# Adding the high part of the residual on VectorE instead of by an identity matmul

## The chip, the cores and the metric

The kernel runs on one core of one Trainium2 chip. The metric is the device time of one execution in microseconds (us), the median of several runs. The names of the engines are those of the profile: PE is TensorE (PEld its weight loads), DVE is VectorE, ACT is ScalarE, POOL is GpSimd, SP is SyncE, which issues most of the plain transfers.

## The reference

Input x is 4 images of 512 channels, 32 x 32 pixels, fp32. Four layers follow each other:

```
layer 0  h = relu(bn(conv1x1 512->128)); offsets = conv3x3(h); h = deformable conv3x3(h, offsets)
         x = relu(bn(conv1x1 128->512 of relu(bn(h))) + x)
layer 1  25 local self-correlations of x, normalised; x = relu(conv1x1 (512+25)->512 of [x, correlations])
layer 2  h = relu(bn(conv1x1 512->128)); h = relu(bn(conv3x3 128->128)); x = relu(bn(conv1x1 128->512) + x)
layer 3  the same shape as layer 2 with other weights; its x is the output
```

What the change touches is the last line of layers 2 and 3: `relu(W3 h + b + x)`, 512 output channels in 4 blocks of 128, for each half (512 pixels) of the image. One block of one half is an "expand" step: 4 blocks x 2 halves x 2 layers = 16 a image, 64 in all.

## The kernel before

Values of layers 1 to 3 are kept as two fp32r parts, a high part and a low part (value minus high part); a product of two such values is three matmuls, high x high, low x high, high x low (`product`, L544 to L548). So each tile of 128 x 512 is left in this order: PE accumulates it in a PSUM bank; ACT applies scale, bias and relu into a slot of `ring` (4 slots, L806); ACT copies the slot to the high part (L810); DVE subtracts the high part from the slot to get the low part (L1069, items called "fine").

An expand step on PE is five matmuls of 128 x 128 by 512 columns: two by the identity `ident_r` (L665), which bring the high and the low part of the residual `xs` into the bank, and the three of the product. For layer 2 ACT and DVE then do the three operations above. For layer 3 there are no parts: the first half is drained by ACT alone (L806), the second half by DVE alone (L1076, bias and relu in one TENSOR_SCALAR), into a ring slot from which SP stores it.

The order of all work is written out by hand in `ROWS` (L80 to L95) and put together by `row_items` (L98). A row has steps of layers 1 to 3 of one image and, in the same row, a unit u of layer 0 of the image after it (18 units: two halves x nine taps) and possibly one output block of layer 0. Every engine walks the same list of items in this order and does its part of each, so an engine that waits in one item holds all that follow. The items of a row, in order: `weigh(u+1)` on ACT (4 tiles times a weight, L841) with `blend(u+1)` on DVE (12 operations, L1047); `outhigh` of an earlier block on ACT (L859, L862); the steps; `turn(u)` (PE transposes `samp`, L691; ACT copies to `sampT`, L847); the "fine" of the row's last step on DVE; `outlow` (DVE, L1063); `tap(u-1)` (PE, L701); `out0` (PE L711, DVE L1055). The "fine" of a step that isn't the last one of its row stands behind the step after it.

The expands of layer 2 stand in the rows `(2,0,0) (2,0,1)` with unit 11, `(2,0,2) (2,0,3)` with no unit, `(2,1,0) (2,1,1)` with unit 13, then `reduce(3,0)` with unit 14, then `(2,1,2) (2,1,3)` with no unit. `reduce(3,0)` waits for the "fine" of `(2,0,3)`, `reduce(3,1)` for that of `(2,1,3)`. The eight expands of layer 3 stand in pairs in the last four rows, each with an output block of layer 0.

POOL gathers the patches of layer 0 by indirect DMA, 4 to a unit, two units ahead, into 12 slots that blends free (L512 is its wait, L514 the gather). PE has four banks for the steps (`BANK`); a bank is free when `c_drained` of its step four earlier has come. The prologue (layer 0 of image 0) ends at about 176 us; three passes of the loop (layers 1 to 3 of images 0 to 2, beside layer 0 of images 1 to 3) run to 343, 519 and 690 us; the epilogue, layers 1 to 3 of image 3 alone, to the end.

Of the kernel before, what the change touches and what calls it, by code (L numbers as in the profile page):

```python
# [7 lines left out]
KC = C // P  # L8
HALF = HW // 2
# [43 lines left out]
BANK = [n % C_BANKS for n in TAKE]  # L53
# [134 lines left out]
def drains(ic, c):  # L188

    return ic * BANK_USES[BANK[c]] + TAKE[c] // C_BANKS + 1  # L190
# [18 lines left out]
def conv_seq_kernel(nc, x, w1t, offwt, offb, w2t, w3t, l1wt, l1gt, l2w1t, l2w2t, l2w3, l3w1t, l3w2t, l3w3,  # L209
# [17 lines left out]
    with ctx:  # L227
# [7 lines left out]
        def sem(name):  # L235
            return ctx.enter_context(nc.semaphore(name))
# [100 lines left out]
        out0_done, res_summed, res_relu, x1_high, x1_low = (  # L337
            sem(n) for n in ("out0_done", "res_summed", "res_relu", "x1_high", "x1_low"))
        ld_res = [sem(f"ld_res{n}") for n in range(RES)]
        c_done = sem("c_done")  # L340
        c_drained = [sem(f"c_drained{b}") for b in range(C_BANKS)]
        corr_step, norm_asked, norm_root, gs_done = (
            sem(n) for n in ("corr_step", "norm_asked", "norm_root", "gs_done"))
# [51 lines left out]
        def _(sp):  # L395
# [24 lines left out]
            def body(items, ib, ic):  # L420
# [3 lines left out]
                for it in items:  # L424
# [31 lines left out]
                    if it[0] == "step" and C_STEPS[it[1]][:2] == ("expand", 3):  # L456
                        _, _, h, m = C_STEPS[it[1]]
                        c = it[1]
                        sp.wait_ge(c_drained[BANK[c]], drains(ic, c) + 1)
                        sp.dma_start(out_v[ic, m, :, h * HALF:(h + 1) * HALF], slot(c))\  # L460
                          .then_inc(stored[RING_USE[c] % RING], 16)

# [80 lines left out]
        def _(pe):  # L543
# [79 lines left out]
            def step(c, ic):  # L623
# [15 lines left out]
                elif s[0] == "corrT":  # L639
                    h = s[1]  # L640
                    pe.wait_ge(gs_done, 6 * ic + 3 * h + 3)
                    for t in range(HT):
                        last = pe.transpose(ps[0:3 * PART, t * P:(t + 1) * P],
                                            gs[:, t].rearrange("p a b -> p (a b)"), ident)
                elif s[0] == "mix":
                    _, h, m = s
                    ct = STEP_AT[("corrT", h)]
                    pe.wait_ge(c_drained[BANK[ct]], drains(ic, ct) + 1)
                    last = pe.matmul(ps[:], l1g[:, m * P:(m + 1) * P], gsT[:], start=False, stop=True)
                elif s[0] == "reduce":  # L650
                    _, layer, h = s
                    source = [STEP_AT[("mix", h, m) if layer == 2 else ("expand", 2, h, m)] for m in range(KC)]
                    pe.wait_ge(fine_done, fined(ic, max(source, key=FINE_AT.get)))
                    for k in range(KC):
                        last = product(ps[:], [wr[layer][p][:, k, :] for p in range(2)],
                                       [xs[p][:, k, h * HALF:(h + 1) * HALF] for p in range(2)], k == 0, k == KC - 1)
                elif s[0] == "conv":
                    _, layer, h = s
                    pe.wait_ge(fine_done, fined(ic, STEP_AT[("reduce", layer, 1)]))
                    last = conv_taps(c, range(FIRST_TAPS, TAPS))  # L660
                elif s[0] == "expand":
                    _, layer, h, m = s
                    pe.wait_ge(fine_done, fined(ic, STEP_AT[("conv", layer, h)]))
                    for p in range(2):
                        pe.matmul(ps[:], ident_r[:], xs[p][:, m, h * HALF:(h + 1) * HALF], start=p == 0, stop=False)  # L665
                    last = product(ps[:], [we[layer][p][:, m * P:(m + 1) * P] for p in range(2)],
                                   [h2[p][:, h, :] for p in range(2)], False, True)
                last.then_inc(c_done, 1)
# [56 lines left out]
        def _(act):  # L725
            def col(n):
                return prm[:, n:n + 1]
# [39 lines left out]
            def step(c, ic):  # L767
                s = C_STEPS[c]
                ps = bank[BANK[c]]
                if s[0] == "gram":  # L770
# [9 lines left out]
                            ins.then_inc(aligned, 1)  # L780
                    ins.then_inc(c_drained[BANK[c]], 1)
                    return
                if s[:3] == ("expand", 3, 1):
                    return
                if s[0] == "corrT":
                    act.wait_ge(c_done, NC * ic + c + 1)
# [1 line left out]
                    return  # L788
                value, high, _ = split_parts(c)
                sc = 1.0  # L790
                if s[0] == "expand":
                    _, layer, h, m = s
                    b = col(L3_B3 + m) if layer == 3 else bn[:, 3, 2 + m:3 + m]
                elif s[0] == "mix":
                    _, h, m = s
                    b = col(L1_B + m)
                elif s[0] == "reduce":
# [6 lines left out]
                act.wait_ge(c_done, NC * ic + c + 1)  # L804
                shaped = ps[:] if len(value.shape) == 2 else ps[:].rearrange("p (a b) -> p a b", b=W)
                act.activation(value, shaped, ACT.Relu, bias=b, scale=sc).then_inc(c_drained[BANK[c]], 1)  # L806
                if s[:2] == ("expand", 3):
                    return
                act.wait_ge(c_drained[BANK[c]], drains(ic, c) + 1)
                act.activation(high, value, ACT.Copy).then_inc(step_high, 1)  # L810

# [65 lines left out]
        def _(dve):  # L877
# [123 lines left out]
            def body(items, ib, ic):  # L1001
                for it in items:
# [62 lines left out]
                    elif it[0] == "fine":  # L1065
                        c = it[1]
                        value, high, low = split_parts(c)
                        dve.wait_ge(step_high, len(SPLIT_STEPS) * ic + HIGH_AT[c] + 1)
                        dve.tensor_tensor(low, value, high.bitcast(fp32), ALU.subtract).then_inc(fine_done, 1)  # L1069
                    elif it[0] == "step":  # L1070
                        c = it[1]
                        s = C_STEPS[c]
                        if s[:3] == ("expand", 3, 1):
                            slot_free(dve, ic, c)
                            dve.wait_ge(c_done, NC * ic + c + 1)
                            dve.tensor_scalar(slot(c), bank[BANK[c]][:], prm[:, L3_B3 + s[3]:L3_B3 + s[3] + 1], 0.0,  # L1076
                                              ALU.add, ALU.max).then_inc(c_drained[BANK[c]], 1)
                        elif s[0] == "corrT":

                            dve.wait_ge(gsT_high, 2 * ic + s[1] + 1)  # L1080
# [66 lines left out]
```

## Time and profile before

| what | us |
|---|---|
| median of 3 runs | 770.78 |
| lowest, highest | 753.77, 781.69 |
| span of the profiled execution | 791.2 |
| PE, PEld busy in it | 626.6, 445.0 |
| DVE, ACT, POOL busy in it | 439.6, 366.1, 363.9 |

The three runs lie 28 us apart, and the profiled execution is another one, longer than each of them. Its trace shows what waits for what. "Idle before" of an instruction is time that its engine spent waiting, and the name behind the arrow is what ended it; "remote" or "another core or an unknown queue" is a wait whose release came without a recorded instruction beside it (here only one core runs).

### The profile page before, as it was taken

The page shows a single profiled execution, that of the slowest core. Times are in us where ns is not written, and L with a number is a line of the kernel's source. Part 1 is how long each engine was busy: PE and PEld are TensorE (multiplying, and loading weights), DVE is VectorE, ACT ScalarE, POOL GpSimd, SP SyncE. Part 2 cuts the span into 40 slices and gives each one's busy share as a digit, 9 for nine tenths or more (in the row PEclk, how much of TensorE's full clock was granted, in tenths as well). Part 3 has the DMA queues.
Part 4 walks back from the last instruction along what each step waited for, and adds up shares of the span by engine and source line. Part 5 has one row for each costly group of instructions (what it writes and reads, how often), then busy time and mean ns, then how long its engine had stood idle before and what let it go on. Part 6 is the DMA issues. An engine that isn't in the chain of part 4 may idle for free.

```text
span 791.2 us, 9836 instructions
## 1 busy us (share of the span) xinstructions
PE 626.6 (79%) x2560; PEld 445.0 (56%) x2560; DVE 439.6 (56%) x1295; ACT 366.1 (46%) x762; POOL 363.9 (46%) x453
## 2 busy tenths in 40 slices
PE   6659776467976878994966958995869488999988
PEld 3445362127743656682744636683647366787766
DVE  2437469762885567453964547464848276444222
ACT  3125235642642456552543366552626175545442
POOL 1485665816486863035585852044778750000000
PEclk9977795767997979997987969996979879999999
DMA  8695894516255643165264632164465630400002
GB/s 309 194 307 193 319 310 118 150 36 200 68 163 160 175 134 115 41 212 161 70 186 133 174 115 82 68 205 138 113 179 144 199 109 25 138 9 1 0 1 106
DMA packets 46947, 109.94 MB, mean 139 GB/s; under 512 B 6575, under 2 KB 14831, under 8 KB 46778
## 3 DMA queue, kind: packets, MB, share of 16 engines
q0 software_dynamic: 23040, 75.52, 32.3%
q1 hardware_dynamic: 23866, 34.00, 12.6%
q8 instruction: 11, 0.18, 0.1%
q14 instruction: 30, 0.25, 0.1%
HBM read 96.94 MB, written 12.55 MB: 138 GB/s over the span
## 4 chain that ended last, share of the span: by engine, by line
PE 50%; another core or an unknown queue 14%; issue 12%; POOL 11%; ACT 6%; DVE 4%; DMA 3%; ACTq 0%; SPq 0%; DVEq 0%; POOLq 0%
PE bank L546 10%; PE bank L548 10%; PE bank L547 10%; POOL patch L514 9%; PE bank L701 6%; PE bank L665 4%; PE bank L563 3%; PE bank L691 2%; PE bank L711 2%; ACT ring L806 2%; POOL tick L512 2%; ACT samp L841 1%; DVE samp L1047 1%; DMA patch<-patch_tables,idx 1%
## 5 line engine op out<-in xcount | busy, mean ns | idle before, releaser
L1047 DVE SCALAR_TENSOR_TENSOR samp<-patch,wgt,samp 128x128 f32<-128x128 f32 x864 | 237.1, 346 | 92.1 <-ACT samp L841 58.5
L514 POOL DMA_INDIRECT patch<-patch_tables,idx x216 | 220.2, 1019 | 50.1 <-issue 36.3
L512 POOL TENSOR_TENSOR tick<-tick 1x1 f32<-1x1 f32 x144 | 60.9, 423 | 211.2 <-DVE wgt L1031 120.6
L701 PE MATMUL bank<-sampT,w 128*128 128x512 f32 x144 | 91.1, 719 | 44.8 <-ACT sampT L847 34.5
L841 ACT ACTIVATE samp<-patch,wgt 128x128 f32<-128x128 f32 x288 | 93.5, 392 | 24.7 <-DMA patch<-patch_table,idx 16.2
L691 PE MATMUL bank<-ident_r,samp 128*128 128x128 f32 x288 | 50.7, 299 | 48.1 <-DVE samp L1047 42.3
L514 POOL DMA_INDIRECT patch<-patch_table,idx x72 | 77.0, 1070 | 16.8 <-issue 12.0
L847 ACT ACTIVATE sampT<-bank 128x512 f32<-128x512 f32 x72 | 42.2, 587 | 83.5 <-remote 46.4
L1069 DVE TENSOR_TENSOR xs_low<-ring,xs_high 128x512 fp32r<-128x512 f32 x64 | 43.1, 689 | 66.3 <-ACT xs_high L810 48.8
L806 ACT ACTIVATE ring<-bank,prm 128x512 f32<-128x512 f32 x64 | 44.2, 701 | 77.0 <-PE bank L548 29.8
L691 PEld LDWEIGHTS bank<-ident_r,samp 128*128 128x128 f32 x288 | 38.3, 153 | 71.3 <-DVE samp L1047 56.3
L546 PE MATMUL bank<-x_high,l1w_high 128*128 128x512 f32 x128 | 59.7, 466 | 10.3 <-issue 5.3
L806 ACT ACTIVATE ring<-bank,bn 128x512 f32<-128x512 f32 x48 | 34.0, 708 | 61.7 <-remote 36.0
L548 PE MATMUL bank<-x_high,l1w_low 128*128 128x512 f32 x128 | 54.3, 424 | 1.8 <-issue 1.8
L777 ACT ACTIVATE corr<-bank 32x320 f32<-32x320 f32 x64 | 27.4, 428 | 60.9 <-remote 38.7
L547 PE MATMUL bank<-x_low,l1w_high 128*128 128x512 f32 x128 | 54.3, 424 | 1.0 <-issue 1.0
L701 PEld LDWEIGHTS bank<-sampT,w 128*128 128x128 f32 x144 | 25.8, 221 | 51.4 <-ACT sampT L847 39.3
L563 PE MATMUL bank<-xa,w 128*128 128x512 f32 x64 | 37.7, 721 | 13.5 <-issue 7.9
L859 ACT ACTIVATE res<-res,prm 128x512 f32<-128x512 f32 x32 | 23.1, 721 | 48.5 <-DVE res L1055 48.4
L546 PE MATMUL bank<-x_high 128*128 128x256 f32 x128 | 37.6, 294 | 6.0 <-ACTq L869 4.1
L810 ACT ACTIVATE xs_high<-ring 128x512 fp32r<-128x512 f32 x64 | 40.4, 631 | 2.0
L548 PE MATMUL bank<-x_high,x_low 128*128 128x256 f32 x128 | 37.8, 296 | 1.4 <-issue 1.4
(168 smaller groups left out, 1214.9 us busy)
## 6 DMA issues: line engine op xcount, KB each, us to landing
res<-in_x SPq DMA_DIRECT2D x32, 256.0 KB
out_y<-ring SPq DMA_DIRECT2D x32, 256.0 KB, 2.1
xa<-in_x SPq DMA_DIRECT2D x7, 1024.0 KB, 7.3
patch<-patch_tables,idx POOLq DMA_INDIRECT x216
patch_tables<-midT SPq DMA_DIRECT2D x11, 256.0 KB
patch<-patch_table,idx POOLq DMA_INDIRECT x72
xa<-in_x SPq DMA_DIRECT2D x4, 256.0 KB, 4.9
xa<-in_l1wt SPq DMA_DIRECT2D x1, 1024.0 KB
```

Source lines behind the costliest of these rows:

```text
L512: pool.tensor_tensor(tick[:, p:p + 1], tick[:, 0:1], tick[:, 0:1], ALU.add).then_inc(ticked, 1)
L514: pool.indirect_dma_start(patch[:, n % SLOTS].rearrange("p a c -> p (a c)"), None, table, bass.IndirectOffsetOnAxis(ap=idx[:, e:e + 1], ax ...
L546: pe.matmul(ps, w[0], a[0], start=start, stop=False)
L547: pe.matmul(ps, w[0], a[1], start=False, stop=False)
L548: return pe.matmul(ps, w[1], a[0], start=False, stop=stop)
L563: last = pe.matmul(bank[h][:], w1[:, c, :], xa[i % 2][:, c, h * HALF:(h + 1) * HALF], start=c == 0, stop=c == KC - 1)
L691: last = pe.transpose(bank[4 + u % 2][:, t * P:(t + 1) * P], samp[:, u % 2, t, :], ident)
L701: pe.matmul(bank[6 + h][:], w2[:, k, :], sampT[:, u % 2, :], start=k == 0, stop=k == TAPS - 1).then_inc(tap_done, 1)
L806: act.activation(value, shaped, ACT.Relu, bias=b, scale=sc).then_inc(c_drained[BANK[c]], 1)
L841: act.activation(samp[:, u % 2, t, :], patch[:, n % SLOTS, 0, :], ACT.Copy, scale=wgt[:, (HT * h + t) * TAPS + k, 0:1]).then_inc(weighed, 1)
L1047: dve.scalar_tensor_tensor(o_, g_, w_, o_, ALU.mult, ALU.add).then_inc(blended, 1)
L1069: dve.tensor_tensor(low, value, high.bitcast(fp32), ALU.subtract).then_inc(fine_done, 1)
```

## The change

PE's expand step has four matmuls: the identity matmul for the low part alone, and the product. DVE drains the bank for all 16 expands of an image: one SCALAR_TENSOR_TENSOR adds bank, bias and the high part of the residual into the ring slot, without relu. ACT then reads the slot: for layer 2 it writes relu of it straight into the high part of `xs`; for layer 3 it applies relu in place and signals a new semaphore `final`, on which SP's store waits. The "fine" of a layer 2 expand on DVE becomes a SCALAR_TENSOR_TENSOR: max of the slot with 0, minus the high part.

```
 PE    pe.wait_ge(fine_done, fined(ic, STEP_AT[("conv", layer, h)]))
-      for p in range(2):
-          pe.matmul(ps[:], ident_r[:], xs[p][:, m, h * HALF:(h + 1) * HALF], start=p == 0, stop=False)
+      pe.matmul(ps[:], ident_r[:], xs[1][:, m, h * HALF:(h + 1) * HALF], start=True, stop=False)
 ACT
-      if s[:3] == ("expand", 3, 1):
+      if s[0] == "expand":
+          act.wait_ge(c_drained[BANK[c]], drains(ic, c) + 1)
+          if s[1] == 3:
+              act.activation(slot(c), slot(c), ACT.Relu).then_inc(final, 1)
+          else:
+              act.activation(split_parts(c)[1], slot(c), ACT.Relu).then_inc(step_high, 1)
           return
 DVE, fine
+      if C_STEPS[c][0] == "expand":
+          dve.scalar_tensor_tensor(low, value, 0.0, high.bitcast(fp32), ALU.max, ALU.subtract)\
+             .then_inc(fine_done, 1)
+      else:
           dve.tensor_tensor(low, value, high.bitcast(fp32), ALU.subtract).then_inc(fine_done, 1)
 DVE, step
-      if s[:3] == ("expand", 3, 1):
+      if s[0] == "expand":
+          _, layer, h, m = s
+          b = prm[:, L3_B3 + m:L3_B3 + m + 1] if layer == 3 else bn[:, 3, 2 + m:3 + m]
           slot_free(dve, ic, c)
           dve.wait_ge(c_done, NC * ic + c + 1)
-          dve.tensor_scalar(slot(c), bank[BANK[c]][:], prm[:, L3_B3 + s[3]:L3_B3 + s[3] + 1], 0.0,
-                            ALU.add, ALU.max).then_inc(c_drained[BANK[c]], 1)
+          dve.scalar_tensor_tensor(slot(c), bank[BANK[c]][:], b,
+                                   xs[0][:, m, h * HALF:(h + 1) * HALF].bitcast(fp32),
+                                   ALU.add, ALU.add).then_inc(c_drained[BANK[c]], 1)
 SP
-      sp.wait_ge(c_drained[BANK[c]], drains(ic, c) + 1)
+      sp.wait_ge(final, 2 * KC * ic + KC * h + m + 1)
       sp.dma_start(out_v[ic, m, :, h * HALF:(h + 1) * HALF], slot(c))
```

## Rows read from the trace of the kernel before

**Rows 1.** Page, busy us, share of the span and instructions of each engine.

```profile
PE 626.6 (79%) x2560; PEld 445.0 (56%) x2560; DVE 439.6 (56%) x1295; ACT 366.1 (46%) x762; POOL 363.9 (46%) x453
```

**Rows 2.** Chain of waits that ended last, its start and two stretches: start, us, what.

```profile
466.73 0.85 PE bank L665 x2
...
478.66 0.46 PE bank L665 x2
...
578.90 12.81 another core or an unknown queue
```

**Rows 3.** Stretches: window, us, busy of PE, PEld, DVE, ACT, POOL; clock, DMA.

```profile
612.00:636.00 24.00, 11.26 (x47) 7.81 (x46) 7.52 (x25) 5.83 (x14) 15.56 (x22) 0.83 0.61 175
636.00:652.00 16.00, 16.00 (x60) 11.54 (x59) 14.35 (x44) 13.29 (x28) 11.73 (x12) 0.83 0.43 122
744.00:792.00 48.00, 41.07 (x171) 31.53 (x169) 12.01 (x17) 19.46 (x30) 0.00 (x0) 1.00 0.12 44
```

**Rows 4.** Timeline of PE, third pass: start, us, engine, line, form, idle before.

```profile
622.57 0.60 PE L691 MATMUL bank<-ident_r,samp 128*128 128x128 f32 x4
635.50 2.08 PE L701 MATMUL bank<-sampT,w 128*128 128x512 f32 x2 [12.33 <-ACT sampT L847]
```

**Rows 5.** Groups of instructions: form, count, busy us, mean ns, idle before.

```profile
L665 PE MATMUL bank<-xs_high,ident_r 128*128 128x512 f32 x64 | 35.7, 558 | 0.1
L806 ACT ACTIVATE ring<-bank,bn 128x512 f32<-128x512 f32 x48 | 34.0, 708 | 61.7 <-remote 36.0 <-PE bank L548 23.3 <-issue 1.5
L810 ACT ACTIVATE xs_high<-ring 128x512 fp32r<-128x512 f32 x64 | 40.4, 631 | 2.0
L859 ACT ACTIVATE res<-res,prm 128x512 f32<-128x512 f32 x32 | 23.1, 721 | 48.5 <-DVE res L1055 48.4
L1055 DVE SCALAR_TENSOR_TENSOR res<-bank,prm,res 128x512 f32<-128x512 f32 x32 | 23.9, 746 | 4.8 <-PE bank L711 3.1 <-DMA res<-in_x 1.5
L1069 DVE TENSOR_TENSOR xs_low<-ring,xs_high 128x512 fp32r<-128x512 f32 x64 | 43.1, 689 | 66.3 <-ACT xs_high L810 48.8 <-issue 17.5
L1076 DVE TENSOR_SCALAR ring<-bank,prm 128x512 f32<-128x512 f32 x16 | 12.0, 751 | 7.4 <-PE bank L548 7.4
```

**Rows 6.** Timeline of DVE, second pass, blends and "fines" around the layer 2 expands.

```profile
469.29 0.69 DVE L1063 TENSOR_TENSOR x_low<-res,x_high 128x512 fp32r<-128x512 f32 x1
...
472.40 0.69 DVE L1069 TENSOR_TENSOR xs_low<-ring,xs_high 128x512 fp32r<-128x512 f32 x1 [1.43 <-issue]
473.01 3.29 DVE L1047 SCALAR_TENSOR_TENSOR samp<-patch,wgt,samp 128x128 f32<-128x128 f32 x12
476.21 1.29 DVE L1069 TENSOR_TENSOR xs_low<-ring,xs_high 128x512 fp32r<-128x512 f32 x2
477.42 3.24 DVE L1047 SCALAR_TENSOR_TENSOR samp<-patch,wgt,samp 128x128 f32<-128x128 f32 x12
480.57 0.69 DVE L1069 TENSOR_TENSOR hp_low<-ring,hp_high 128x512 fp32r<-128x512 f32 x1
```

**Rows 7.** Timeline of ACT and PE in the same stretch of the second pass.

```profile
475.92 0.58 ACT L847 ACTIVATE sampT<-bank 128x512 f32<-128x512 f32 x1
...
477.64 1.02 PE L701 MATMUL bank<-sampT,w 128*128 128x512 f32 x2
...
485.22 0.50 PE L546 MATMUL bank<-xs_high,l3w_high 128*128 128x512 f32 x1 [2.08 <-DVE xs_low L1069]
```

**Rows 8.** Timeline of PE, third pass, the last two of four output blocks of layer 0.

```profile
683.65 1.02 PE L711 MATMUL bank<-hid,w 128*128 128x512 f32 x2
686.84 1.02 PE L711 MATMUL bank<-hid,w 128*128 128x512 f32 x2
```

**Rows 9.** Timeline of the epilogue: the last layer 2 expands and the end.

```profile
761.28 0.69 DVE L1069 TENSOR_TENSOR xs_low<-ring,xs_high 128x512 fp32r<-128x512 f32 x1 [0.54 <-ACT xs_high L810]
762.12 0.47 PE L546 MATMUL bank<-xs_high,l3w_high 128*128 128x512 f32 x1 [2.57 <-DVE xs_low L1069]
...
787.83 0.75 DVE L1076 TENSOR_SCALAR ring<-bank,prm 128x512 f32<-128x512 f32 x1 [0.41 <-PE bank L548]
```

More of the change, by code:

```diff
@@ L339, in conv_seq_kernel @@
         ld_res = [sem(f"ld_res{n}") for n in range(RES)]
-        c_done = sem("c_done")
+        c_done, final = sem("c_done"), sem("final")
         c_drained = [sem(f"c_drained{b}") for b in range(C_BANKS)]
@@ L790, in step @@
                 sc = 1.0
[L791 to L794, printed above, removed]
+                if s[0] == "mix":
                     _, h, m = s
@@ L806, in step @@
                 act.activation(value, shaped, ACT.Relu, bias=b, scale=sc).then_inc(c_drained[BANK[c]], 1)
-                if s[:2] == ("expand", 3):
-                    return
                 act.wait_ge(c_drained[BANK[c]], drains(ic, c) + 1)
@@ L1068, in body @@
                         dve.wait_ge(step_high, len(SPLIT_STEPS) * ic + HIGH_AT[c] + 1)
-                        dve.tensor_tensor(low, value, high.bitcast(fp32), ALU.subtract).then_inc(fine_done, 1)
+                        if C_STEPS[c][0] == "expand":
+                            dve.scalar_tensor_tensor(low, value, 0.0, high.bitcast(fp32), ALU.max,
+                                                     ALU.subtract).then_inc(fine_done, 1)
+                        else:
+                            dve.tensor_tensor(low, value, high.bitcast(fp32), ALU.subtract).then_inc(fine_done, 1)
                     elif it[0] == "step":
```

## The prediction

> **What bounds the kernel now.** I read busy shares first: PE 79%, DVE 56%, ACT and POOL 46% [rows 1]. That says which engine to look at, not what its work is worth. The chain of waits comes next. In it the expands of layer 2 in a pass of the loop are a run of PE pieces: the two identity matmuls of one expand take 0.85 us at the half clock and 0.46 us at full clock [rows 2], so a removed one is worth 0.43 or 0.23 us where PE is the chain. But the chain also has pieces as in 578.90, 12.81 us that no recorded instruction ended [rows 2]. The stretches show where these lie: from 612 to 636 us PE is busy for 11.26 of 24 us, DVE for 7.52, ACT for 5.83, and POOL, which only issues gathers, for 15.56 [rows 3]. PE had issued the transposes of unit 12 at 622.57 and then stood for 12.33 us until ACT had copied them [rows 4]. Here PE's work costs nothing. Then 636 to 652 us: PE 16.00 of 16 us, DVE 14.35, ACT 13.29 [rows 3]. Here PE is the chain, but with DVE and ACT right behind it, and this is where six of the eight layer 2 expands lie. From 652 on, and through the epilogue, PE is mostly the chain at full clock.
>
> So the change takes work from PE and gives it to DVE at a place where DVE has 1.65 us to spare.
>
> **Part 1, PE.** 64 identity matmuls go. Their mean of 558 ns [rows 5] holds pipelining; the step between matmuls is 0.23 us, and 0.43 at half clock [rows 2]. All of them: 64 x 0.23 = 14.7 us, and 0.2 us more for each at half clock, perhaps 8 of them, 1.6 us: 16.3 us, if nothing else were late.
>
> **Part 2, the price of the new operations.** The drain on DVE is a SCALAR_TENSOR_TENSOR of 128x512 from PSUM with a second tensor from SBUF. L1055 is this very form: 746 ns [rows 5]. ACT's relu from the slot is not shown for this pair of types; the Copy L810 has 631 ns and the relu with bias L859 721 ns [rows 5]; I take 0.67. The new "fine" with max is not shown either: between the TENSOR_TENSOR, 689 ns, and L1055, 746 ns; I take 0.69, as both its inputs are in SBUF as there [rows 5]. For the three such operations that lie on the chain of one image the two ends are less than 0.2 us apart.
>
> A layer 2 expand costs before: ACT 0.71 + 0.63 and DVE 0.69; after: DVE 0.75 + 0.69 and ACT 0.67 [rows 5]. A layer 3 expand before: one drain of 0.7 (ACT in the first half, L806; DVE in the second, L1076); after: DVE 0.75 and ACT 0.67. DVE gains 12 operations an image, 12 x 0.75 x 4 = 36 us in all. The chain from c_done to the low part of a single expand stays as long as it was (0.71 + 0.63 + 0.69 against 0.75 + 0.67 + 0.69). For a pair it gets shorter: ACT was the slower one at 1.34 a tile; now DVE does drain, drain, fine, fine, 4 x 0.69 to 0.75 = 2.9 us, with ACT beside it, against 3.4. SP's wait moves from the drain to the relu; nothing but stores stands behind it.
>
> **Part 3, layer 2 in a pass.** The pair with unit 11 comes out of the stall of the gathers, and both chains have one length: nothing gained or lost. For the other three pairs I walk through DVE's list in the second pass.
> - (2,0,2), (2,0,3): before, the last fine ran from 472.40 to 473.09, and blend(14) began at 473.01 [rows 6]. DVE is free from 469.98, where its outlow ends [rows 6]. Drain, drain, fine, fine takes it to 472.8 to 473.0. Blend(14) starts where it did.
> - (2,1,0), (2,1,1): blend(14) ends at 476.3. ACT could drain these tiles during the blend; DVE can't. Two drains now stand behind it, 476.3 to 477.8, then ACT's relu to 478.4. Only behind that relu comes ACT's copy of sampT for unit 13: 478.4 to 479.0, where it ran from 475.92 to 476.50 [rows 7]. That is 2.5 us late. PE's tap 13, which began at 477.64 [rows 7], begins at 479.0, 1.4 us late, although PE saved 2 x 0.43 + 2 x 0.23 = 1.3 us before it: PE stands for 2.5 us.
> - ACT's weigh(15) follows sampT, so blend(15), which ran from 477.42 [rows 6], begins at 479.4 and ends at 482.6, and the fine of reduce(3,0) (at 480.57 before [rows 6]) ends at 483.3.
> - (2,1,2), (2,1,3): drain, drain, fine, fine, 483.3 to 486.2. reduce(3,1) begins at 486.2, where it began at 485.22 [rows 7]. **Loss 1.0 us a pass**, with every saving of PE in these rows gone into waits.
>
> In the third pass the same steps give a loss of 0.9 to 1.1.
>
> **Part 4, layer 3 in a pass.** The last four rows come 3.19 us apart [rows 8], all PE: two expands of 1.16 and an output block of 0.86. After: 2.72. DVE does two drains, an outlow and an out0 in each, 0.75 + 0.67 + 0.60 + 0.75 = 2.77, as they follow one another without a gap; ACT 2 x 0.67 + 0.72 + 0.63 = 2.7. All three level, so I take 2.8: 4 x 0.4 = **1.6 us gained a pass**. Three passes: 3 x (1.0 - 1.6) = -1.8 us.
>
> **Part 5, epilogue.** No layer 0 work covers anything here: DVE is busy for 12.01 of the last 48 us, PE for 41.07 [rows 3]. Before, reduce(3,1) started at 762.12 behind a fine that began at 761.28 [rows 9]. The same walk (PE 0.93 an expand, DVE 2.9 a pair, conv(2,1) moved up by 0.5) gives 762.4: +0.3. The conv steps don't change. The eight expands of layer 3 give 8 x 0.23 = 1.84 us back on PE. At the end a tile was out 0.75 us after its drain began (787.83 [rows 9]) and stored 2.6 us later (791.2 less 788.6); now 0.7 of relu comes between. A ring slot is then held for 0.75 + 0.7 + 2.6 = 4.0 us while PE makes four tiles in 3.7: +0.4. Sum: 0.3 - 1.84 + 0.7 + 0.4 = **-0.4 us**.
>
> **Sum.** -1.8 - 0.4 = -2.2 us of 791.2, so 789. The profiled execution is 2.6% longer than the median of 770.78, and the runs spread from 753.77 to 781.69. Scaled by 0.974: **768.6 us**, no change that could be told (I count 2%, 15.4 us, as what can be told). Bounds of this case by itself: PE's 0.23 saved on all of the passes' last rows and part of the layer 2 ones, 6 us less; the losses of part 3 without the gains of part 4, 5 us more; 763 to 776.
>
> **A rule against a row.** The share of the span is the measure by which PE at 79% comes out as the engine to relieve, and yet 636 to 652 us shows DVE at 14.35 of 16 us [rows 1, 3]. The Trainium skill, page "Perfetto Trace Analysis", section "Identifying the Most-Contended Engine", says that for TensorE the matmul busy share is no good measure and the share of weight loads is to be taken. By it PE (56%) and DVE (56%) would be level before, and after the change DVE, at about 60%, would lead: nothing gained, or something lost. The trace agrees with this where the layer 2 expands lie, and not in the last rows of a pass, where PE without a gap sets the pace.
>
> **Rivals.**
> *PE's saving gets through.* If PE is the chain nearly everywhere (its busy time is 626.6 [rows 1], and the chain has PE in every expand) and DVE's drains fit between blends, all of part 1 counts: -16.3 + 0.7 at the end = -15.6, that is 775.6, scaled 755. For it: PE without a gap from 636 to 652 [rows 3]. Against it: DVE's 14.35 there has no room for four drains, and the pair in the shadow of unit 11 is worth nothing. Chance 0.14.
>
> *Slower: PE's pauses pull its clock down.* Place: tap 13 and reduce(3,1). PE's pause before reduce(3,1) was 2.08 us, in the epilogue 2.57 [rows 7, 9], and the clock stayed at 2.4 GHz. After 12.33 us of standing it was at 1.2 GHz: identity matmuls of 0.43 us [rows 2, 4]. After the change PE stands for 2.5 us at tap 13 and for 3 to 4 us at reduce(3,1), close to each other. If this is enough, the reduce and conv steps behind it run at half speed for some time; the mean of 0.83 over 636 to 652 us [rows 3] is 1/3 of the time at half level, 5.3 us, in which 2.7 us of work are lost. Two such stretches an image, one behind each pause, with the loss of part 3 and the gain of part 4: 4 x (2 x 2.7 + 1.0 - 1.6) = 19, so 810, scaled 789; with one stretch an image 779. It decides from the point at which pauses of 3 to 4 us, not 2.6, bring the clock down. Chance 0.12.
>
> *The gaps of the gathers move.* Waits like the 12.81 us that nothing recorded ended [rows 2] come where POOL issues gathers back to back [rows 3], some two or three a pass. The change shifts blends by 2 us, and blends free the gathers' slots. One such gap more or less in one pass is 13 us; in every pass 38 us. The runs before lie 28 us apart, most likely for this reason. Nothing in the trace says to which side: 0.06 for more than 13 us faster, 0.06 for slower.
>
> *The relief of ACT counts.* ACT loses 8 operations of layer 2 and gains 4 in layer 3 an image. It leads only if ACT was the bound; its share of 46% and part 3, where it waits for DVE, speak against it. Inside the forecast's own range.
>
> **How the numbers follow.** Forecast 0.62, saving gets through 0.14, clock 0.12, gaps 0.12. Faster by over 2%: half of the case at 755, which lies on the border (0.07), the gaps to that side (0.06), and 0.03 for the spread of the runs: 0.16. Slower by over 2%: the clock case with both stretches (0.06), the gaps (0.06), 0.02 for the spread: 0.14. Within: 0.70. Range: 752 to 786, which takes in the 755 of the one rival and all but the far end of the other, and the spread of a median of such runs.
>
> **What would show it.** In the profile after: L665 with 64 instead of 128 matmuls; DVE about 473 us busy, PE about 36 less than 626.6 by the records. Step 3 is right if PE stands for 2 to 3 us before tap 13 (L701) with ACT's sampT as releaser, and reduce(3,1) waits longer than 2.08 for DVE; wrong if tap 13 comes directly behind the transposes. Step 4 is right if L711 comes 2.8 us apart in the last rows. Step 5 is right if the last store ends less than 1 us earlier, counted from reduce(2,0) of the epilogue. The clock rival shows as a granted clock under 1.00 in the 30 us behind reduce(3,1). The forecast is wrong as a whole if the last 55 us of a pass change by over 3 us.

## The result and the profile after

| set of runs | kernel before, median us | changed kernel, median us | ratio, 95% interval |
|---|---|---|---|
| first | 769.96 (753.77 to 784.88) | 769.25 (760.69 to 782.97) | 1.0124 (1.0069 to 1.0180) |
| second | 783.05 (776.13 to 794.70) | 785.79 (777.64 to 793.12) | 1.0021 (0.9976 to 1.0066) |
| third | 785.25 (775.51 to 798.33) | 784.36 (776.12 to 1412.3) | 0.9994 (0.9945 to 1.0043) |

The forecast of 768.6 us and "no change" came out in the median, and its sign did not: I had 2 us to the good; the first interval says 0.7 to 1.8% slower, the other two hold no change. The ratio of the first set compares the runs within 1.5% of the fastest of each kernel, which are 4 of 20 before and 13 of 20 after, since the kernel before spread more. The medians of all runs in it are 0.7 us apart, with the changed kernel the lower one. So no change of 2% was there, a loss of up to 1.8% may have been, and taking 64 matmuls from PE bought nothing. The page after, with its chain by engine:

```profile
PE 611.5 (80%) x2496; PEld 432.6 (56%) x2496; DVE 469.2 (61%) x1343; ACT 356.4 (46%) x746; POOL 365.9 (48%) x453
...
PE 33%; DVE 17%; issue 17%; another core or an unknown queue 10%; POOL 10%; ACT 8%; DMA 4%; DVEq 1%; SPq 0%; ACTq 0%; POOLq 0%
```

Against [rows 1], PE has 64 matmuls and 15.1 us less and DVE 29.6 us more. That is near 64 steps of 0.23 us (14.7), and not the 36 us that the prediction read off the records: PE's records overlap, and the identity matmul that is left, now the first of its group, has 554 ns where it had 411. The groups that answer to [rows 5] (form, count, busy us, mean ns, idle before):

```profile
L664 PE MATMUL bank<-xs_low,ident_r 128*128 128x512 f32 x64 | 35.5, 554 | 3.2 <-DVE h_low L1072 1.8 <-issue 1.3
L1081 DVE SCALAR_TENSOR_TENSOR ring<-bank,bn,xs_high 128x512 f32<-128x512 f32 x32 | 22.6, 742 | 8.5 <-remote 5.0 <-PE bank L548 3.4
L1069 DVE SCALAR_TENSOR_TENSOR xs_low<-ring,xs_high 128x512 fp32r<-128x512 f32 x32 | 21.7, 692 | 0.7
L787 ACT ACTIVATE xs_high<-ring 128x512 fp32r<-128x512 f32 x32 | 20.2, 631 | 45.7 <-DVE ring L1081 29.8 <-issue 15.5
L785 ACT ACTIVATE ring<-ring 128x512 f32<-128x512 f32 x32 | 18.7, 619 | 3.0 <-DVE ring L1081 2.8
```

The prices were right: drain 742 ns for 0.75, fine 692 for 0.69, relu 619 to 631 for 0.67. DVE in the second pass, where [rows 6] stood (start, us, engine, line, form):

```profile
456.77 3.23 DVE L1046 SCALAR_TENSOR_TENSOR samp<-patch,wgt,samp 128x128 f32<-128x128 f32 x12
459.92 1.40 DVE L1081 SCALAR_TENSOR_TENSOR ring<-bank,bn,xs_high 128x512 f32<-128x512 f32 x2
461.36 1.35 DVE L1069 SCALAR_TENSOR_TENSOR xs_low<-ring,xs_high 128x512 fp32r<-128x512 f32 x2
462.79 3.27 DVE L1046 SCALAR_TENSOR_TENSOR samp<-patch,wgt,samp 128x128 f32<-128x128 f32 x12
465.98 0.68 DVE L1072 TENSOR_TENSOR hp_low<-ring,hp_high 128x512 fp32r<-128x512 f32 x1
466.59 1.40 DVE L1081 SCALAR_TENSOR_TENSOR ring<-bank,bn,xs_high 128x512 f32<-128x512 f32 x2
468.02 1.35 DVE L1069 SCALAR_TENSOR_TENSOR xs_low<-ring,xs_high 128x512 fp32r<-128x512 f32 x2
```

No idle time stands in any of these rows: from 456.8 to 469.4 DVE's list is the clock of the kernel. The timelines of ACT and PE there, beside [rows 7]:

```profile
460.70 1.29 ACT L787 ACTIVATE xs_high<-ring 128x512 fp32r<-128x512 f32 x2 [3.40 <-issue]
461.89 0.58 ACT L846 ACTIVATE sampT<-bank 128x512 f32<-128x512 f32 x1
...
462.52 1.13 PE L700 MATMUL bank<-sampT,w 128*128 128x512 f32 x2 [1.81 <-DVE xs_low L1069]
...
469.43 0.50 PE L546 MATMUL bank<-xs_high,l3w_high 128*128 128x512 f32 x1 [0.93 <-DVE xs_low L1069]
```

The sampT copy stands right behind the two relus and ends at 462.47, and tap 13 starts at 462.52, with PE idle for 1.81 us, where it had come without a wait. (The row names a "fine" of DVE as the releaser; what tap 13 waits for in the program is sampT.)

A pass can be cut by rows of PE: the first matmul of the correlations (gram), of reduce(2,0), of reduce(3,0), of reduce(3,1), and gram again. Lengths of these stretches in us, three passes each, from the traces of this case:

| kernel | gram to reduce(2,0) | to reduce(3,0) | to reduce(3,1) | to gram |
|---|---|---|---|---|
| before | 62.1, 64.3, 62.9 | 59.5, 65.6, 62.6 | 11.91, 11.20, 11.21 | 34.1, 34.1, 34.0 |
| before, profile of the third set | 61.9, 63.5, 63.8 | 59.5, 59.9, 59.8 | 11.43, 11.27, 9.60 | 35.6, 35.6, 34.1 |
| changed | 60.7, 62.5, 61.3 | 59.0, 54.0, 55.0 | 12.56, 12.53, 12.58 | 33.5, 33.5, 33.4 |
| changed, second set | 61.9, 62.5, 61.8 | 60.7, 60.0, 60.5 | 12.57, 12.58, 12.58 | 33.5, 33.6, 33.5 |

Stretches one and two vary by several us from profile to profile of either kernel; that is where the 23.7 us between the two first profiles lie, and nothing is read from it. Stretch three is longer in the changed kernel every time, and always the same. Stretch four is shorter. The two values of 35.6 in the third set's profile hold a stretch of low clock right behind reduce(3,1) (granted clock 0.68 from 306.7 to 312.0 us in the first pass), to which PE came after 2.29 and 2.14 us of idle time; the changed kernel stands there for 0.93 us (second pass) and shows no low clock behind it in the nine passes of its three full profiles.

### The profile page after: what moved, and what is told of

It reads as the page before. It is cut to its first block, busy times and chain, and to the rows that moved or that the text cites. A ratio compares the mean times of both kernels' runs of the same rounds, so it can differ in the third digit from the quotient of the medians.

```text
span 767.5 us, 9731 instructions
## 1 busy us (share of the span) xinstructions
PE 611.5 (80%) x2496; PEld 432.6 (56%) x2496; DVE 469.2 (61%) x1343; ACT 356.4 (46%) x746; POOL 365.9 (48%) x453
## 3 DMA queue, kind: packets, MB, share of 16 engines
q0 software_dynamic: 23040, 75.52, 33.4%
## 4 chain that ended last, share of the span: by engine, by line
PE 33%; DVE 17%; issue 17%; another core or an unknown queue 10%; POOL 10%; ACT 8%; DMA 4%; DVEq 1%; SPq 0%; ACTq 0%; POOLq 0%
DVE samp L1046 8%; POOL patch L514 8%; PE bank L546 8%; PE bank L548 7%; PE bank L547 7%; PE bank L700 3%; PE bank L563 3%; DVE ring L1081 2%; POOL tick L512 1%; PE bank L690 1%; ACT samp L840 1%; DMA out_y<-ring 1%; PE bank L710 1%; ACT ring L807 1%
## 5 line engine op out<-in xcount | busy, mean ns | idle before, releaser
L700 PE MATMUL bank<-sampT,w 128*128 128x512 f32 x144 | 88.5, 702 | 37.2 <-ACT sampT L846 20.1
L840 ACT ACTIVATE samp<-patch,wgt 128x128 f32<-128x128 f32 x288 | 95.2, 392 | 40.4 <-DMA patch<-patch_tables,idx 19.3
L807 ACT ACTIVATE ring<-bank,prm 128x512 f32<-128x512 f32 x48 | 34.0, 709 | 42.0 <-PE bank L548 21.5
L563 PE MATMUL bank<-xa,w 128*128 128x512 f32 x64 | 34.9, 683 | 10.1 <-DMA xa<-in_x 5.9
L787 ACT ACTIVATE xs_high<-ring 128x512 fp32r<-128x512 f32 x32 | 20.2, 631 | 45.7 <-DVE ring L1081 29.8
L710 PE MATMUL bank<-hid,w 128*128 128x512 f32 x64 | 36.7, 665 | 2.6 <-DVE res L1054 1.6
L547 PE MATMUL bank<-x_low,x_high 128*128 128x256 f32 x128 | 37.6, 294 | 0.8 <-issue 0.7
```

Source lines behind the costliest of these rows:

```text
L547: pe.matmul(ps, w[0], a[1], start=False, stop=False)
L563: last = pe.matmul(bank[h][:], w1[:, c, :], xa[i % 2][:, c, h * HALF:(h + 1) * HALF], start=c == 0, stop=c == KC - 1)
L700: pe.matmul(bank[6 + h][:], w2[:, k, :], sampT[:, u % 2, :], start=k == 0, stop=k == TAPS - 1).then_inc(tap_done, 1)
L710: pe.matmul(bank[b][:], w3[:, m * P:(m + 1) * P], hid[:], start=True, stop=True)\
L840: act.activation(samp[:, u % 2, t, :], patch[:, n % SLOTS, 0, :], ACT.Copy, scale=wgt[:, (HT * h + t) * TAPS + k, 0:1]).then_inc(weighed, 1)
```

## The experiments

**1 to 4. Without the gathers.** The gathers' waits cover everything of a few us, so POOL writes ones into each slot instead of gathering; then the change, and each half of it, are timed.

```
-  pool.indirect_dma_start(patch[:, n % SLOTS]..., None, table, ...).then_inc(gathered[n % SLOTS], 16)
+  pool.memset(patch[:, n % SLOTS], 1.0).then_inc(gathered[n % SLOTS], 1)
```

The kernel before without gathers was expected so:

> The kernel before, with each gather of layer 0's patches replaced by a fill of the same slot with ones on GpSimd (this part of the result is left out; every other instruction is kept). If the waits that nothing recorded ended (13.8% of the chain, some two or three a pass) belong to the gathers, they are gone from the trace, the time falls by about 100 us from 770 to 650 to 690, and the runs lie within 3 us of each other instead of 28. If they belong to something else (code loading, ScalarE, semaphores), they stay.

The changed kernel without gathers:

> The changed kernel with the same replacement. Theory (VectorE's in-order list sets the pace of the layer 2 expands, and its lag eats most of the layer 3 gain): 2 to 5 us slower than the kernel before with the same replacement, from +1.0 to +1.7 a pass in layer 2, -0.65 a pass in layer 3 and +1.0 in the epilogue. Rival A (TensorE's saving gets through): 8 to 16 us faster. Rival B (only the gaps of the gathers moved): within 1 us.

Only the eight expands of layer 2 an image changed (each part of the diff under `if s[:2] == ("expand", 2)`):

> No gathers, and only the expands of layer 2 changed. Theory: 3 to 7 us slower than the kernel before without gathers (three passes at +1.0 to +1.7, the epilogue at 0 to +1.7 by the clock). Rival A: 6 to 8 us faster (32 matmuls at 0.23).

Only those of layer 3 changed:

> No gathers, and only the expands of layer 3 changed. Theory: 2 to 4 us faster than the kernel before without gathers (three passes at -0.7 to -1.1 since VectorE starts its drains behind a fine and an output block, the epilogue at -0.7). Rival A: 7 us faster (32 matmuls at 0.23).

Measured (stretches from the profiles), with the kernel before at 782.28 us beside them:

| without gathers | median us (lowest, highest) | reduce(2,0) to reduce(3,0) | to reduce(3,1) | to gram | epilogue |
|---|---|---|---|---|---|
| before | 637.27 (636.02, 638.34) | 36.9 | 9.23 | 34.0 | 101.1 |
| changed | 648.83 (646.96, 649.27) | 37.6 | 12.52 | 33.5 | 103.4 |
| layer 2 alone | 651.58 (650.21, 652.00) | 37.6 | 12.52 | 34.0 | 103.6 |
| layer 3 alone | 637.86 (637.62, 638.27) | 36.9 | 9.23 | 33.5 | 101.7 |

With the gathers gone the kernel before takes 637 us, below the 650 to 690 that I had expected, and its runs lie 2.3 us apart. The change costs 11.6 us (1.8%) here, all of it layer 2's. Both sizes that I gave for it, 2 to 5 and 3 to 7, were too small; layer 3 alone, from which I expected 2 to 4 us, gave nothing (0.6 us slower). The rival by which PE's saving arrives is dead: with PE at 91% of the span, it would have shown here if anywhere.

In the two profiles, which lie 13.4 us apart, the difference is 3 x 3.3 us in stretch three, 3 x 0.7 in the stretch before it, 3 x 0.5 back in the one behind it, and 2.3 in the epilogue; the rest is in the prologue and in stretch one, whose length changes with the low clock that falls into it (49.4 to 53.7 us over all profiles without gathers). Stretch three, reduce(3,0) to reduce(3,1) in the second pass, as windows (us, busy of PE, PEld, DVE, ACT, POOL; clock, DMA), first before, then changed:

```profile
357.64:366.86 9.22, 9.17 (x38) 5.95 (x37) 8.69 (x27) 8.78 (x19) 3.24 (x6) 1.00 0.00 1
```

```profile
363.42:375.95 12.53, 10.45 (x36) 6.58 (x35) 12.37 (x34) 7.13 (x17) 2.25 (x6) 0.86 0.00 0
```

Before, PE has 9.17 of 9.22 us, ACT 8.78 and DVE 8.69: three engines level. The change puts 3.7 us more on DVE there: four drains of 0.70, and 0.8 us of blend(14), which begins 0.1 us ahead of reduce(3,0) and no longer 0.9. So DVE has 12.37 of 12.53 us. (The clock of 0.86 costs nothing: the passes at full clock have 12.53 and 12.52 us too.)

**5 to 7. DVE's order, or DVE's load?** One kernel lets DVE do the drains of expand(2,1,0) and (2,1,1) ahead of blend(14):

```
+  pair = [("step", STEP_AT[("expand", 2, 1, m)]) for m in range(2)]
+  at = items.index(("blend", 14, 0));  items = items[:at] + pair + items[at:]     # DVE's list only
```

> The changed kernel, gathers replaced by a write of ones into the slot (that part of the result is left out). Only VectorE's order is changed: its two drains of the tiles of expand(2, 1, m) stand ahead of blend(14) and not behind it. Reference 648.8 us for the changed kernel and 637.3 us for the kernel before, both without gathers. Theory 'order' (TensorE waits because a drain stands behind 3.3 us of blends, then sampT(13) behind the relu): most of the +3.3 us a pass from reduce(2, 1)'s tiles to reduce(3, 1) comes back, 1.5 us a pass or more, time 644 us or less. Theory 'load' (VectorE has no idle time from the first drain of layer 2 to reduce(3, 1), so that each operation moved forward moves another back): under 0.5 us a pass, time 647 to 650 us.

Measured: 648.07 us (647.96 to 650.44), stretch three 12.14 us for 12.52. Only 0.4 us a pass came back. The other two take load away:

```
-  g_ = patch[:, (HT * u + t) % SLOTS, corner, :];    o_ = samp[:, u % 2, t, :]
+  wide_ = 8 if u in (14, 15) and corner > 1 else P
+  g_ = patch[:, (HT * u + t) % SLOTS, corner, 0:wide_];    o_ = samp[:, u % 2, t, 0:wide_]
```

> The changed kernel without gathers, 16 of its blend operations a pass narrowed from 128 to 8 columns (those of units 14 and 15, corners 2 and 3; their sum is left out of the result). Everything keeps its place and its waits; VectorE has some 2 us a pass less to do between the drains of layer 2 and reduce(3, 1). Theory 'load': time falls from 648.8 by 1.5 to 2 us a pass, to 643 or less (-5 to -7 with the prologue's and epilogue's rows). Theory 'order' with TensorE as the bound behind it: about half of that, 646 or more.

> Control for the last: the kernel before without gathers, the same 16 blend operations a pass narrowed to 8 columns. Theory 'load': in the kernel before VectorE does not set the pace between the drains of layer 2 and reduce(3, 1), so the time stays within 2 us of 637.3. If it falls by as much as the changed kernel's (5 us or more), VectorE set the pace in both and the change only lengthened its list by its own work.

Measured: changed 639.99 us (639.34 to 641.45), stretch three 10.55; before 634.71 us (633.63 to 636.68), stretch three 9.23 in all three passes, as it was. The 2.6 us that it lost on the median, 0.6 more than the 2 that I had allowed, show in its trace as the third pass, 129.7 us for 132.1, and not in the stretch of the blends: the profile of the kernel before has 6.8 us at the lower clock in stretch one of that pass, and this one has none. In the changed kernel DVE's busy time in stretch three fell by 1.97 us (12.37 to 10.40) and the stretch by 1.97; in the kernel before it is worth nothing there. (Runs 5 to 8 were taken on another chip than 1 to 4; stretch two of the changed kernel has 37.6 us on both.) The loss in stretch three is DVE's load, by experiment.

**8, 9. The clock in the epilogue.** Windows of the changed kernel without gathers, around reduce(3,1), which came behind 3.26 us of idle PE:

```profile
608.00:615.00 7.00, 4.90 (x20) 3.67 (x20) 4.87 (x9) 3.49 (x6) 0.00 (x0) 1.00 0.00 0
615.00:622.00 7.00, 5.68 (x13) 4.46 (x14) 1.18 (x2) 0.57 (x2) 0.00 (x0) 0.54 0.01 2
```

The granted clock of 0.54 is the lower level, 1.2 GHz, for nearly the whole window. The experiment gives PE something to do before that wait:

```
+  if isinstance(ic, int) and ic == N - 1 and s == ("reduce", 3, 1):
+      pe.wait_ge(sampT_done, UNITS * N)
+      for _ in range(8): pe.matmul(bank[5][:], ident_r[:], h2[0][:, 1, :], start=True, stop=True)
```

> The changed kernel without gathers, with 8 matmuls of 128x512 added in the epilogue ahead of reduce(3, 1)'s wait, in a free PSUM bank that nobody reads, so that TensorE does not stand for 3.3 us there. Theory 'clock': the stretch of 6.8 us at the lower clock behind that pause goes away, and time falls from 648.8 by 2 to 3.4 us. Rival (the stretch costs nothing, since VectorE and ScalarE end the epilogue): within 1 us of 648.8.

> The changed kernel with 8 matmuls of 128x512 added in the epilogue ahead of reduce(3, 1)'s wait, in a free PSUM bank that nobody reads. Without gathers this took away a stretch of 6.8 us at the lower clock and 2.8 us. In the first profile of the changed kernel that stretch was 3.4 us. Theory: 1.5 to 3 us less than the changed kernel of this set; rival (the clock falls there for another reason): within 1 us.

Measured without gathers: 646.0 us (643.39 to 646.28, and one run of 725.02), 2.8 less; the window of reduce(3,1) now, with PE idle only for 1.29 us before reduce(3,1):

```profile
614.00:621.00 7.00, 5.71 (x25) 4.28 (x24) 2.23 (x4) 2.24 (x4) 0.00 (x0) 1.00 0.00 0
```

With gathers its median of 785.94 us (ratio to the kernel before 1.0004, 0.9952 to 1.0057) can't be told from the changed kernel's 785.79, so that expectation was not borne out; in the two traces the epilogue from gram on is 100.6 us for 103.2, and 2.6 us is below what those runs can resolve.

**10, 11. Only the four tiles that DVE drained anyway.** `NEW = s[:3] == ("expand", 3, 1)`: PE's matmul goes, and DVE's list doesn't grow.

> The same edit as in the run with gathers (only the four tiles of expand(3, 1, m)), with the gathers replaced by a write of ones into the slot, which is left out of the result. Reference 637.3 us for the kernel before without gathers, 637.9 with all eight tiles of layer 3 changed. Theory: 633.5 to 635.5 us (three passes by 0.9, one epilogue by 0.9 less 0.7). Rival (VectorE's drains pace the rows): 637 to 638.

> Only the four tiles of expand(3, 1, m) are changed, which VectorE drained in the kernel before too: its drain takes the high part of the residual instead of the relu, TensorE drops four identity matmuls of 0.23 us a pass, and ScalarE adds a relu in place. VectorE's list does not grow. Theory: TensorE's saving of 0.9 us a pass arrives where layer 3's rows set the pace, less what the relu adds behind the last drain (0.7 us once at the end): 2 to 4 us less than the kernel before at 680 us, and not to be told from no change at 770. Rival (the rows of layer 3 are paced by VectorE's drains whoever adds the residual): within 1 us.

Measured: 638.3 us without gathers (636.32 to 638.95, and one run of 828.23), 782.71 with them, ratio 0.9990 (0.9947 to 1.0033). I had expected 633.5 to 635.5 without gathers. Nothing gained, so no version of the idea that was run beat the kernel before. Its pass ends 33.5 us behind reduce(3,1), 0.5 less, and its epilogue is 102.3 for 101.1, with a stretch of low clock behind reduce(3,1) that the profile of the kernel before doesn't have.

**12 to 18. Where the loss goes when there are gathers.** The changed kernel again in full, twice, the kernel before once with a profile, the pair with every second gather (odd n) replaced by ones, and the pair with all gathers spaced by three 1x1 additions on POOL ahead of each.

> The changed kernel as it is, beside the kernel before. The kernel before took 770, 782 and 680 us in three earlier sets of runs, and 637 without gathers: how much the gathers hold up the signals of the other engines differs from set to set. Theory (the loss of 3.3 us a pass is VectorE's list, and what of it is not seen is hidden by that disturbance): if the kernel before takes 674 to 690 us here, the change costs 7 to 12 us (1.0 to 1.8%); if it takes 765 or more, 0 to 9 us. Rival (the cost without gathers is a property of those kernels alone): within 4 us at either level.

> The changed kernel once more, for the level of the kernel before on this set's chip (so far 770, 782, 783 and once 680 us). Theory (the loss of 3.3 us a pass is hidden where the gathers hold up the other engines' signals): with the kernel before at 674 to 690 us the change costs 7 to 12 us; at 765 or more it costs 0 to 9 us. Rival: the change costs less than 4 us at either level.

> The kernel before (all the change's edits off), for a profile of it on this set's chip. Both theories: a ratio of 0.995 to 1.005. If the level is 680 us, its trace has no stretches of 10 to 22 us without a signal from TensorE in layer 2; at 770 or more it has.

> The kernel before with every second gather (odd tiles of 128 positions) replaced by a write of ones into its slot, the rest as it is; those parts of the result are left out. Without any gather 637.3 us, with all of them 783 us on the chips that were slow. Theory: a level between, 660 to 720 us.

> The changed kernel with every second gather replaced in the same way. Theory (the cost is 11.6 us without disturbance and nearly nothing with all of it): 5 to 11 us above the kernel before with half of the gathers. Rival (the cost depends on the gathers being there at all): within 4 us of it.

> The kernel before with all its gathers and its full result, and three additions of 1x1 on GpSimd ahead of each gather, so that gathers are issued about 1.8 us apart and not 1.28. With every second gather left out (1.67 us apart at the closest, and half the bytes) the kernel before took 641 us. If the closeness of the issues is what holds up the other engines' signals: well below the 783 to 785 us of the last sets, 650 to 740. If it is the number of gathers or their bytes: 775 to 800.

> The changed kernel with the same three additions ahead of each gather. Theory (the change's loss of 3.3 us a pass shows where signals are not held up, whether or not all gathers are there): if the spaced kernel before falls below 740 us, this one takes 5 to 12 us more than it; if that stays at 775 or more, within 5 us of it.

The two full runs are in the table above (the kernel before came out at 1.0017 of itself, 0.9974 to 1.0060). The others:

| pair | before us | changed us | difference | stretch three before, changed |
|---|---|---|---|---|
| no gathers | 637.27 | 648.83 | 11.6 | 9.23, 12.52 |
| half of them | 641.40 | 652.96 | 11.6 | 9.22, 12.52 |
| all, second set | 783.05 | 785.79 | 2.7 | 9.6 to 11.9, 12.5 to 12.6 |
| all, spaced | 799.49 | 800.50 | 1.0 | 12.3 to 13.1, 12.7 to 13.5 |

The difference is the same with half of the gathers, so their being there does not hide it. Two expectations were missed here: with half of the gathers the kernel before came to 641 and not to 660 to 720, and the difference lies just above the 5 to 11 that I had given. In the third set the difference is -0.9 us. The spaced pair ran on a chip on which the kernel before takes 682 us. Spacing failed as a probe: POOL's own list of 1305 instructions became the bound, 60% of the chain of waits:

```profile
POOL 60%; issue 19%; PE 16%; DVE 2%; DMA 1%; ACT 1%; SPq 0%; POOLq 0%; DVEq 0%; ACTq 0%
```

What hides part of the loss with all gathers stands in the kernel before's own trace: its last matmul of expand(2,1,2) and ACT's drain of it, first with gathers, then without (timelines of PE and ACT):

```profile
479.43 0.39 PE L548 MATMUL bank<-h_high,l2w_low 128*128 128x512 f32 x1
...
481.85 0.69 ACT L806 ACTIVATE ring<-bank,bn 128x512 f32<-128x512 f32 x1 [2.37 <-PE bank L548]
```

```profile
363.06 0.39 PE L551 MATMUL bank<-h_high,l2w_low 128*128 128x512 f32 x1
...
363.49 0.69 ACT L817 ACTIVATE ring<-bank,bn 128x512 f32<-128x512 f32 x1 [0.28 <-PE bank L551]
```

2.42 us from one to the other, and 0.43. With all gathers issued back to back, PE's signal came 2.0 us late, ACT drained late, and stretch three was 11.2 us instead of 9.2. In the chain of waits PE's signal comes at 481.83, and ACT starts 0.02 us behind it:

```profile
480.75 1.08 PE bank L548
481.83 0.02 issue
481.85 0.70 ACT ring L806
```

The trace's record of that semaphore shows the signals of both expands there, at 481.83 and 481.90, though their last matmuls began 1.16 us apart (479.43 and 480.59). In the third set's profile the time from matmul to drain is 2.49 us (471.20 to 473.69). In the third pass of the kernel of run 11 the signal was in time:

```profile
642.54 0.39 PE L553 MATMUL bank<-h_high,l2w_low 128*128 128x512 f32 x1
...
642.97 0.69 ACT L819 ACTIVATE ring<-bank,bn 128x512 f32<-128x512 f32 x1 [0.52 <-PE bank L553]
```

and that stretch has 9.22 us. In the changed kernel the stretch has 12.53 to 12.58 us with gathers and 12.52 without. Its three full profiles don't show the late signal at this place: in eight of their nine passes the record of the second expand's signal stands 0.41 or 0.42 us behind its matmul (the ninth has no record). Nor would it have cost much, since the drain stands behind twelve blend operations anyway and begins 2.4 us behind the matmul (464.18 to 466.59). Why the signals come in time there was not tested. So 3.3 us a pass is the price, 2.0 of it was being paid before the change for another reason in most passes, and 1.3 shows.

## Why the prediction was right or wrong

The value, 768.6 for 769.25 us, is luck: it is the level of three runs with 2 us taken off, and the same kernel before came out between 770 and 785 us in the sets above. The forecast was about the difference, and its terms gave 2.2 us to the good. Without gathers, where they can be read, they measure 3 x (3.3 + 0.7 - 0.5) + 2.3 = 12.8 us to the bad in the profiles, 11.6 in the medians.

**Parts 1 and 2** held: 64 matmuls gone at a step of 0.23 us, prices within 0.05 us. What the prediction called the point of it, that a removed PE instruction is worth nothing where DVE stands behind it, held too.

**Part 3 is the step that failed.** The place and the order of waits came as written (idle 1.81 us before tap 13 for the forecast 2.5), but "loss 1.0 us a pass" was measured at 3.3 for stretch three without gathers and 0.7 more between reduce(2,0) and reduce(3,0), and at 1.3 in most passes with gathers (12.57 less 11.2), where the 0.7 can't be read. Two things were wrong. The first bullet's "Blend(14) starts where it did" has it at DVE's old time, but DVE has two drains more to do before it: without gathers it starts 37.5 us behind reduce(2,0) for 36.0. And the walk from there to reduce(3,1), 13.2 us, was long enough (12.66 measured, with gathers and without), but what I held against it, 12.2 us from 473.01 to 485.22, is 10.1 without gathers. I started each walk from the times of one profiled execution and took them for the work's own. In [rows 6] DVE's fines at 476.21 and 480.57 looked like places with slack; the 2.37 us by which ACT waited for PE at 481.85 were no slack of the schedule but a late signal. The undisturbed stretch has DVE at 8.69 of 9.22 us, and adding four drains to such a list costs all of their 2.8 us.

**Part 4** was mis-sized: 33.5 for 34.0, a gain of 0.5 us a pass and not 1.6. The rows did come closer, 2.73 us apart for 3.19 [rows 8], but DVE started them late and PE waited for its last drains (DVE, then PE, third pass of the changed kernel):

```profile
654.85 0.69 DVE L1072 TENSOR_TENSOR h_low<-ring,h_high 128x512 fp32r<-128x512 f32 x1 [4.42 <-ACT h_high L809]
655.46 0.74 DVE L1054 SCALAR_TENSOR_TENSOR res<-bank,prm,res 128x512 f32<-128x512 f32 x1
656.12 1.40 DVE L1081 SCALAR_TENSOR_TENSOR ring<-bank,prm,xs_high 128x512 f32<-128x512 f32 x2
...
664.54 1.40 DVE L1081 SCALAR_TENSOR_TENSOR ring<-bank,prm,xs_high 128x512 f32<-128x512 f32 x2
...
661.35 1.02 PE L710 MATMUL bank<-hid,w 128*128 128x512 f32 x2
665.34 0.39 PE L546 MATMUL bank<-x_high 128*128 128x256 f32 x1 [1.11 <-DVE ring L1081]
```

At 2.81 us a row (656.12 to 664.54 in three rows) DVE never caught up, and the correlations of the next image, whose bank such a drain frees, waited 1.11 us. That wait is the difference between 1.6 and 0.5. I had ended the count at the last row and not asked who waits for the drain behind it. The runs bear it out: all of layer 3 gives 0.5 us a pass, and so do its second four tiles alone.

**Part 5** was right but for the clock: from reduce(3,1) to the end 28.3 us with the filler for 29.0 before, a gain of 0.7 where -1.84, +0.7 and +0.4 make 0.7. Without the filler it is 30.0 to 31.2 us. PE idled for 3.26 us there, and the clock fell right behind it (timeline, then the window):

```profile
737.53 0.47 PE L546 MATMUL bank<-xs_high,l3w_high 128*128 128x512 f32 x1 [3.26 <-DVE xs_low L1069]
```

```profile
738.00:742.00 4.00, 4.00 (x13) 3.09 (x12) 0.00 (x0) 0.00 (x0) 0.00 (x0) 0.57 0.02 4
```

**The rivals.** The clock rival cost 1.7 to 2.9 us once, in the epilogue, and not 2.7 eight times. At tap 13 the clock fell too, in five of the fifteen passes of the five profiles of the changed kernel (with all gathers, half and none), and it cost nothing, since DVE set the pace: stretch three has 12.52 to 12.58 us in all of them. At reduce(3,1) of a pass it didn't fall. It is also no property of the change alone: the kernel before has 30.3 us from reduce(3,1) to the end, with such a stretch, in the third set's profile. The gaps of the gathers did move between profiles, by more than the change's effect. "PE's saving gets through" has no run for it. Without gathers DVE was the engine to look at before loading it: 70% busy and PE at 91%, and it was load on DVE that cost. The Trainium skill, page "Perfetto Trace Analysis", section "Identifying the Most-Contended Engine", does not take TensorE's matmul busy share for its measure but the share of weight loads, beside the share of the peak arithmetic rate that the kernel reaches; the weight loads are 66% in that profile, so by them DVE comes first, and the run of the changed kernel agrees (+11.6 us). The run with narrower blends agrees only in part: taking load off DVE left stretch three of the kernel before at 9.23 us, where PE is busy for 9.17.

The sum, put right with gathers: 3 x (1.3 + 0 to 1 - 0.5) - 0.7 + 1.7 to 2.9, that is 3 to 8 us, 0.4 to 1.0% (an estimate from these stretches), in reach of all three intervals. Against the third set's profile, in which the kernel before has its own low clock, stretches three and four together differ by only 0.2 us a pass and the epilogue by 1.0. How much of the first set's 0.7 to 1.8% is the change and how much its wider spread before was not settled. Left open also: the sets ran on different chips, and on two of them the kernel before took 680.48 and 682.3 us; no run of the changed kernel as it is and no profile of the kernel before was taken there, so whether the change costs nearer to 11.6 us on such a chip was not measured.

## What to carry to other kernels

Before moving work to an engine, take its busy time in the stretch where the work lands and ask whether the idle time beside it is the schedule's or a late signal's: a gap that something else makes is no room. Count on to whoever waits for the last moved instruction, here the next image's first matmul. And when a large disturbance blurs a change of 1%, take the disturbance out of both kernels: 11.6 us with runs 2 us apart could be read, 3 us with runs 18 us apart could not.

## What the runs showed of the hardware

The cost of the gathers is not in proportion to their number: 637 us without any, 641 with half of them, 783 with all (on the chips of those runs). Groups of ACT's sampT copies in the kernel before, with all gathers and with every second one:

```profile
L847 ACT ACTIVATE sampT<-bank 128x512 f32<-128x512 f32 x72 | 42.2, 587 | 83.5 <-remote 46.4 <-PE bank L691 37.1
```

```profile
L863 ACT ACTIVATE sampT<-bank 128x512 f32<-128x512 f32 x72 | 42.2, 586 | 35.8 <-PE bank L700 35.8
```

The 46.4 us of "remote" waits are gone with half of them. Both late signals above came 0.9 us after POOL's last gather of a burst had ended (480.02 plus 0.95, then 481.85; 471.84 plus 0.94, then 473.69); why was not tested, and what makes the kernel before take 681 us in two sets, each on a chip of its own, and 783 on two other chips neither. Spacing all gathers by 1x1 additions took that "remote" wait away (3.6 us idle ahead of the sampT copies, all for PE) and still gave 799 us beside 682, since POOL then paced everything.

TensorE's clock fell to 1.2 GHz around reduce(3,1) of the epilogue in all nine profiles where PE had stood 3.26 us before it, and in six of the nine where it had stood 2.56 us, as in this row of the kernel with only layer 3 changed, whose matmul took 0.76 us; with the same pause the kernel before without gathers has 0.48 us.

```profile
607.02 0.76 PE L549 MATMUL bank<-xs_high,l3w_high 128*128 128x512 f32 x1 [2.56 <-DVE xs_low L1084]
```
